# Two-layer transformer kernel, experts' pass: the down product ahead of the turn back, expert numbers read two at a time, the first batch's mix on VectorE, ten table entries moved to the heads

## What is computed

```
x = x + L0_attn(layernorm(x))     # gated recurrence of 6 heads
x = x + L0_ffn(layernorm(x))      # 2 shared experts + 16 routed experts, each token to its top 2
x = x + L1_attn(layernorm(x))     # causal attention, 16 heads of 128
x = x + L1_ffn(layernorm(x))      # gate, up, down weights = table[index], a table of 16 entries
```

```
routed[token] = sum over its 2 experts e of w[token, e] * (silu(x @ wg[e]) * (x @ wu[e])) @ wd[e]
```

## Time and profile before

| | |
|---|---|
| median of 3 runs | 2143.7 us (2142.53 to 2146.38) |
| the profiled execution's own time | 2146.1 us |
| span of the profiled execution | 2144.4 us, granted TensorE clock 0.993 |
| PE busy | 2080.2 us, 97% of the span |
| PEld busy | 1809.7 us, 84% |
| DVE busy | 1641.0 us, 77% |
| ACT busy | 1239.4 us, 58% |
| POOL busy | 590.2 us, 28% |

### The profile page before, as it was taken

One profiled execution on the slowest core, in us unless ns is written; L12 is line 12 of the kernel. 1 busy time (PEld: TensorE's weight loads), 2 busy tenths in 40 slices (PEclk: granted clock), 3 DMA queues, 4 the chain that ended last, 5 costly groups with the idle time before them and its releaser, 6 DMA issues. The chain is left out here.

```text
span 2144.4 us, 36740 instructions
## 1 busy us (share of the span) xinstructions
PE 2080.2 (97%) x12620; PEld 1809.7 (84%) x12620; DVE 1641.0 (77%) x4333; ACT 1239.4 (58%) x3432; POOL 590.2 (28%) x624
## 2 busy tenths in 40 slices
PE   6899999899999999999999999999999999999998
PEld 5777677577788999899899989988998999899887
DVE  6788787888878878768876777787687778767775
ACT  5443432236667666656665666666566666656662
POOL 3314354223133232223123311322231232112210
PEclk9999999999999999999999999999999999999999
DMA  6603021366422121113112211311221122111100
GB/s 193 205 1 104 33 77 48 150 191 199 144 74 60 45 75 55 40 43 97 40 41 71 68 40 40 91 43 44 66 70 40 40 79 60 40 50 45 41 20 20
DMA packets 92840, 154.56 MB, mean 72 GB/s; under 512 B 8688, under 2 KB 56560, under 8 KB 92656
## 3 DMA queue, kind: packets, MB, share of 16 engines
q1 hardware_dynamic: 72192, 121.53, 19.1%
q0 software_dynamic: 6144, 16.79, 2.4%
q10 hardware_dynamic: 14320, 13.90, 1.9%
HBM read 112.85 MB, written 39.32 MB: 71 GB/s over the span
## 5 line engine op out<-in xcount | busy, mean ns | idle before, releaser
L713 POOL TENSOR_TENSOR wo_low<-wraw_o,wo_high 128x256 fp32r<-128x256 f32 x128 | 95.1, 743 | 1141.2 <-ACT wo_high L777 1141.2
L1083 ACT ACTIVATE pr<-bank,negmax 128x128 f32<-128x128 f32 (+3 forms) x512 | 263.1, 527 | 195.4 <-DVE negmax L1645 195.4
L1203 DVE TENSOR_TENSOR p_low<-bank,p_high 128x512 fp32r<-128x512 f32 (+2 forms) x384 | 190.2, 551 | 101.5 <-ACT p_high L777 100.7
L777 ACT ACTIVATE p_high<-bank 128x512 fp32r<-128x512 f32 (+2 forms) x384 | 177.8, 497 | 149.6 <-PE bank L2208 149.6
L1645 DVE CUSTOM_DVE_ANT_0 bank<-bank,causal 128x128 f32<-128x128 f32 (+3 forms) x512 | 234.6, 520 | 1.1 <-PE bank L1832 1.1
L1672 DVE SCALAR_TENSOR_TENSOR xs<-bank,rinv,xs 128x256 f32<-128x256 f32 x512 | 211.7, 474 | 1.2 <-PE bank L1832 1.2
L1830 PE MATMUL bank<-h_high,wqk_high 128*128 128x512 f32 x512 | 202.6, 396 | 0.2 <-DVE h_low L1203 0.2
L1832 PE MATMUL bank<-h_high,wqk_low 128*128 128x512 f32 x512 | 202.5, 396 | 0.0
L1831 PE MATMUL bank<-h_low,wqk_high 128*128 128x512 f32 x512 | 202.4, 395 | 0.0
L1203 DVE TENSOR_TENSOR z_low<-bank,z_high 128x512 fp32r<-128x512 f32 x128 | 88.4, 691 | 130.8 <-ACT z_high L777 130.3
L703 POOL TENSOR_TENSOR wqk_low<-wraw,wqk_high 128x512 fp32r<-128x512 f32 x128 | 165.8, 1295 | 0.1
(11 more groups left out here) (349 smaller groups left out, 6185.8 us busy)
## 6 DMA issues: line engine op xcount, KB each, us to landing
wraw<-in_wpair SPq DMA_DIRECT2D x64, 512.0 KB, 4.0
wraw<-in_wpair SPq DMA_DIRECT2D x64, 256.0 KB, 4.3
wraw_o<-in_wpair SPq DMA_DIRECT2D x64, 256.0 KB, 2.9
tokens_by_expert<-xm SPq DMA_DIRECT2D x10, 1024.0 KB, 10.9
xt<-tokens_by_expert SPq DMA_DIRECT2D x40, 256.0 KB, 3.2
expert_results<-ey ACTq DMA_DIRECT2D x40, 256.0 KB, 3.7
wres<-in_wexp SPq DMA_DIRECT2D x1, 6144.0 KB, 19.7
xs<-x_between_stages SPq DMA_DIRECT2D x8, 512.0 KB, 4.9
```

Source lines behind the costliest of these rows:

```text
L713: pool.tensor_tensor(wo2[e][1][:], wraw_o[r][:, e, :], wo2[e][0][:].bitcast(F32), ALU.subtract).then_inc(s_wo, 1)
L777: sc.activation(dst, src, ACT.Copy, scale=scale).then_inc(done, 1)
L1083: ins = sc.activation(pr[:, i, 0:(i + 1) * P], score(i), ACT.Exp, scale=-1.0, bias=negmax[:, i:i + 1], accum_out=rsum[:, i:i + 1])
L1203: v.tensor_tensor(at(parts[1]), src, high_, ALU.subtract).then_inc(done, 1)
```

## The change

Six edits belong together:

- **PE's order.** In iteration t `tile_down(t-3)` now comes right behind `tile_gate_up(t-1)` (and behind the first batch's turn at t = 80), then the read of the expert numbers, then `tile_turn_back(t-2)`.
- **ACT's order.** `tile_result(t-3)` comes ahead of `tile_turned(t-2)`.
- **NVALUES** is 2 and not 4: 40 reads of two numbers in place of 20 reads of four.
- **The first batch's mix** moves from POOL to DVE, as 8 `scalar_tensor_tensor` at tiles 46 to 53. POOL's low parts of the first heads' weights now wait for the products `eh` of 52, 57, 62, 67 and 72 tiles (`s_ea`).
- **Table entries.** The pass goes up to entry 102 (`PASS_ENTRIES`) and not 112. Heads 0 to 9 now do two entries each, one ahead of `low_probs` and one behind `low_v`; heads 10 to 15 do one, as before. The seventh chunk's converted indices and compares get room in `fsg` and `ft` (bf16), since their old tiles are overlaid in the heads.
- **ACT's wait** in `high_ffn_weights`: for six chunks at n = 0, for seven at n = 6, for eight at n = 7.

```diff
-NVALUES = 4
+NVALUES = 2
+FIRST_MIX = 46
+FIRST_STATS = FIRST_MIX + 2 * NT + 2
+LOW_WEIGHTS = 52
+HEAD_ENTRIES = 10
+PASS_ENTRIES = LATE_CHUNK * LUTN - HEAD_ENTRIES
...
@@ pool
-            pool.wait_ge(s_x1[0], 16)
-            for c in range(2):
-                for i in range(NT):
-                    if c == 0:
-                        pool.wait_ge(s_yg[i], 32)
-                    linked(pool.tensor_scalar(yg[:, i, c, :], yg[:, i, c, :], wts[:, i, c:c + 1], None, ALU.mult))
-                for i in range(NT - 1):
-                    linked(pool.tensor_tensor(xs[0][:, i, :], xs[0][:, i, :], yg[:, i, c, :], ALU.add))
-                pool.tensor_tensor(xs[0][:, NT - 1, :], xs[0][:, NT - 1, :], yg[:, NT - 1, c, :], ALU.add
-                                   ).then_inc(s_mix, 1)
-                pool.wait_ge(s_mix, c + 1)
+            pool.wait_ge(s_ea, LOW_WEIGHTS)
             low_qk_weights(0, 0, 0)
+            pool.wait_ge(s_ea, LOW_WEIGHTS + 5)
             low_qk_weights(1, 1, 0)
+            pool.wait_ge(s_ea, LOW_WEIGHTS + 10)
             low_v_weights(0, 0)
+            pool.wait_ge(s_ea, LOW_WEIGHTS + 15)
             low_v_weights(1, 1)
+            pool.wait_ge(s_ea, LOW_WEIGHTS + 20)
             low_out_weights(0, 0, 0)
@@ scalar
-                if n in (0, LATE_CHUNK):
-                    sc.wait_ge(s_lut, (LATE_CHUNK + n // LATE_CHUNK) * LUTN)
+                if n in (0, LATE_CHUNK - 1, LATE_CHUNK):
+                    sc.wait_ge(s_lut, max(n + 1, LATE_CHUNK - 1) * LUTN)
...
+                if 0 <= t - 3 < NTILE:
+                    tile_result(t - 3)
                 if 0 <= t - 2 < NTILE:
                     tile_turned(t - 2)
-                if 0 <= t - 3 < NTILE:
-                    tile_result(t - 3)
@@ vector
             def equal_of(n):
-                return equal_late if n >= LATE_CHUNK * LUTN else equal[n % 2][:]
+                if n >= LATE_CHUNK * LUTN:
+                    return equal_late
+                return equal_bf_late if n >= PASS_ENTRIES else equal[n % 2][:]
...
                 if g < LUTN:
-                    unpack_to(LATE_CHUNK * LUTN + g + 1)
+                    unpack_to(PASS_ENTRIES + g + 1 + min(g, HEAD_ENTRIES))
                 low_probs(g)
...
                     low_v(g + 2, bank[5][:])
+                if g < HEAD_ENTRIES:
+                    unpack_to(PASS_ENTRIES + 2 * g + 2)
...
             def first_batch(t):
+                c, i = divmod(t - FIRST_MIX, NT)
+                if 0 <= c < 2:
+                    if c == 0:
+                        if i == 0:
+                            v.wait_ge(s_x1[0], 16)
+                        v.wait_ge(s_yg[i], 32)
+                    elif i == 0:
+                        v.wait_ge(s_mix, 1)
+                    ins = v.scalar_tensor_tensor(xs[0][:, i, :], yg[:, i, c, :], wts[:, i, c:c + 1], xs[0][:, i, :],
+                                                 ALU.mult, ALU.add)
+                    if i == NT - 1:
+                        ins.then_inc(s_mix, 1)
...
@@ tensor
+                if 0 <= t - 3 < NTILE:
+                    tile_down(t - 3, experts[t - 3])
                 if t < NTILE and t % NVALUES == 0:
                     experts += nc.values_load_multi_w_load_instructions(
                         expert_row[0:1, t:t + NVALUES], engines=(mybir.EngineType.PE,), min_val=0, max_val=NEXP - 1,
                         bass_reorder=False)[1]
                 if 0 <= t - 2 < NTILE:
                     tile_turn_back(t - 2)
-                if 0 <= t - 3 < NTILE:
-                    tile_down(t - 3, experts[t - 3])
```

More of the change, by code:

```diff
@@ L82 @@
 FIRST_TILES = 32
-FIRST_STATS = 56
+FIRST_MIX = 46
+FIRST_STATS = FIRST_MIX + 2 * NT + 2
+LOW_WEIGHTS = 52
 FIRST_CHAIN = FIRST_STATS + 4
@@ L245, in two_layer_program @@
         equal_late = fts[:, 0:LC]
+        fidx_bf_late = fsgs[:, LC:LC + LC // 2].bitcast(BF16)
+        equal_bf_late = fts[:, LC:LC + LC // 2].bitcast(BF16)
         wraw = [sb(f"wraw{i}", [P, 6 * D]) for i in range(2)]
@@ L1435, in unpack_index @@
                     v.wait_ge(s_leq, LUTN * (c - 1))
-                v.tensor_copy(fidx_bf[c % 2][:], fidxs[:, c, :]).then_inc(s_lidx, 1)
+                v.tensor_copy(index_of(c), fidxs[:, c, :]).then_inc(s_lidx, 1)
             def index_of(c):
-                return fidx_late if c == LATE_CHUNK else fidx_bf[c % 2][:]
+                return {LATE_CHUNK: fidx_late, LATE_CHUNK - 1: fidx_bf_late}.get(c, fidx_bf[c % 2][:])
             def equal_of(n):
-                return equal_late if n >= LATE_CHUNK * LUTN else equal[n % 2][:]
+                if n >= LATE_CHUNK * LUTN:
+                    return equal_late
+                return equal_bf_late if n >= PASS_ENTRIES else equal[n % 2][:]
             def unpack_equal(c, e):
@@ L1449, in unpack_equal @@
                     v.wait_ge(s_fidx[c % 2], 16 * (c // 2 + 1))
-                if c == LATE_CHUNK:
+                if n >= PASS_ENTRIES:
                     v.wait_ge(s_lut, n)
@@ L1780, in entries_until @@
             def entries_until(t):
-                busy = min(max(t + 1 - FIRST_STATS, 0), FIRST_APPLY + NT - FIRST_STATS)
+                busy = min(max(t + 1 - FIRST_MIX, 0), FIRST_APPLY + NT - FIRST_MIX)
                 weight = 2 * (t + 1) - busy
-                return (LATE_CHUNK * LUTN - early) * weight // (2 * NTILE - FIRST_APPLY - NT + FIRST_STATS)
+                return (PASS_ENTRIES - early) * weight // (2 * NTILE - FIRST_APPLY - NT + FIRST_MIX)
             def tile_product(t):
```

## The result

The changed kernel takes **2161.1 us** (median of 5 executions, 2160.0 to 2161.9), the kernel before 2143.7 (5 executions): a ratio of 1.008, 95% interval 1.0065 to 1.0095. It is slower, as forecast, but by 17.4 us where 5.5 were forecast, and lies above the range.

What follows compares the result with a forecast made beforehand. PE was taken as the bound, busy 2080.2 of 2144.4 us. Pass +4.9, its end +0.3 and heads +0.3 sum to 5.5 us: profiled 2151.6, less 2.4 for the median, 2149 us; overall range 2135 to 2153.

Steps and rivals of the forecast that it cites:

- The mechanism of the pass: PE's sequencer waits in order, so the last semaphore ahead of a read sets its lead; 0.34 us stall per read.
- a TENSOR_LOAD of two, I take 0.33, the row itself: Read in the pass: two numbers load as long as four, 0.33 us; 38 reads then cost 12.9 us.
- the shrinking read: Rival: a TENSOR_LOAD of two takes 0.165 us, pass 136.1, kernel 2141.6 us, no change; chance 0.25.
- the hidden read: Rival: reads in the pass are hidden, only slowed ones show; pass 129.4, kernel 2134.9 us; chance 0.20.
- Reads beside POOL: In the pass, four reads beside POOL's work cost 0.65 us more each: +2.6 us, bounds 0 to 4.6.
- the 0.6 taken off for the first read: In the pass, the first read, ahead of a filled pipeline, gets 0.6 us shorter.
- Both the 7.3 and the 2.7 us go: PE's standstill in the pass goes: 7.3 us between turns 39 and 54, 2.7 us at the reads.
- The end of the pass: Last tiles hang on successive ACT copies, one extra hand-over: +0.3 us, bounds 0 and 0.7.
- Ten entries in the heads: Heads 0 to 9 get one more entry each, mostly in DVE's idle time: +0.3 us; without cover 11 us.
- so seven or eight are hidden whole: Of ten entries in the heads, seven or eight fit DVE's idle time before `z_low`; short gaps lose 0.1 to 0.2.
- the heads pay: Rival: `z_low` comes late in all ten heads, up to 11 us, about 2159 us; chance 0.06.
- the pass at +4.9: The pass, turns of tiles 0 to 79, was to take 143.7 us against 138.8, +4.9.

Runs made afterwards that it cites:

- e16: The changed kernel with reads of one number and no second table entry in the heads: 2134.2 us, ratio 0.9952.
- e5: The kernel before with only the first batch's mix on DVE and POOL's later waits: 2146.7 us, ratio 1.0003.
- e2: The changed kernel with no second entries in the heads (112 in the pass): 2153.2 us, ratio 1.0046.
- e8: The kernel before with a read of four numbers at every second tile: 2174.2 us, one execution.
- e9: The kernel before with reads of eight numbers: 2168.9 us, ratio 1.011.
- e4: The kernel before with PE's and ACT's new order alone, reads of four, mix on POOL: 2153.8 us, ratio 1.0046.
- e1: The changed kernel with PE's and ACT's old order in the pass: 2159.9 us, ratio 1.0076.
- e17: The kernel before (old order) with the mix on DVE and reads of one number: 2140.0 us, ratio 0.9978.

## Why the prediction was wrong

**The mechanism of the pass was right, its size was not.** The new order makes the lead that hides a read depend on `ehT`; I laid its end at 0.65 behind the turn, it is 0.64, and the new place covers 0.65 us of a read where I had worked out 0.93 - 0.34 = 0.59. The term that failed is "a TENSOR_LOAD of two, I take 0.33, the row itself", with half of it as the other bound. It takes 0.54, above both ends: I had bounded it by a row of four as if fewer numbers could not take longer. The stall is 0.51 to 0.53 instead of 0.34, 38 reads cost 20 us and not 12.9. The rival of the shrinking read is refuted by the same row, and so is the hidden read. (The figure per register that the shrinking read takes from the Trainium skill, Runtime: NRT & Kernel Launch, Instruction fetch mechanics, is one for loads from HBM; `expert_row` lies in SBUF.)

The Trainium skill, DMA: Bandwidth & Descriptors, Latency and other measured facts, has a floor of about 600 ns, paid less often by unrolling by four. The traces do not bear out the floor: undisturbed loads take 0.30, 0.33 and 0.54 us. They agree that four at once is cheaper by the number, and an estimate with the page's 0.6 would have put the stall at 0.61, closer than mine. But unrolling is no rule in itself here: e16 shows one number in 0.30 us, hidden whole.

**"Reads beside POOL", +2.6: nothing.** The 39 loads of the changed kernel are all between 532 and 567 ns. The slow ones of the earlier trace rows start 0.81 to 1.10 us behind ACT's issue of a store, the other reads of before 0.53 to 0.57 behind it, and e5 has slow ones with POOL idle. So of the 4.7 us that the pass is longer than worked out (148.4 for 143.7), the stalls are +7.1 (20.0 for 12.9), the slow reads -2.6, and the rest is small: the 0.6 taken off for the first read does not show, and the floor is 0.4 lower (1.625 a step and not 1.63).

**"Both the 7.3 and the 2.7 us go": right.** In the changed kernel no step without a read is longer than 1.63 us, tiles 46 to 60 included, and in e16, where reads hide nothing, the one late product from tile 4 on is that of tile 64's step.

**The end of the pass, +0.3: nothing** (e2: 25.7 as before).

**Ten entries in the heads, +0.3: they cost 9.4.** This is the largest miss, and the step is "so seven or eight are hidden whole". I compared an entry's 1.1 us with a mean idle time of 1.24 us. But in that very idle time POOL subtracts, and the earlier trace rows had shown a DVE add at 1.67 beside POOL's subtractions; I used it for the mix and not here. There the entry takes up to 3.1 us. The rival "the heads pay" (up to 11 us, chance 0.06) had the place and nearly the price, but not the reason: the entry starts right behind `low_v`, as planned, and is itself longer, and heads 1, 3 and 9 hide it. That its 2159 lies near the measured 2161.1 is in part luck, since it holds the pass at +4.9 where 9.6 were measured (and by its own terms it is 2160). The Trainium skill, GPSIMD Engine Reference, Specifications, says that GpSimd's SBUF interfaces are shared with VectorE and contend with VectorE's instructions that have two SBUF inputs or run in its two-port mode; the add has two, and the runs agree: 0.78 alone, 1.75 beside POOL, while `z_low`, which reads one input from a bank, stays at 0.69.

Together: +9.6 in the pass (forecast 4.9) and +9.4 behind it (0.6) are 19.0 us between equal stage ones; the medians show 17.4.

**What stays open.** A TENSOR_LOAD in flight about a microsecond behind the issue of a store takes 0.2 to 0.9 us more. What it and the transfer share, no run here shows, and so it is not shown either that the store is the cause and not something that goes with it. Distance, count and POOL alone do not decide it (e8, e9, e5); the registers of gate and up are neither shown nor refuted.

## What to carry over

A sequencer's read of values costs its engine only what exceeds the lead at its place: work out the lead from the last wait ahead of it, measure the read at that very count, start and place, and make it short enough (one number at a time, 0.64 us, is free here behind a lead of 0.65). Idle time of DVE is worth its length only where POOL is idle too, so take an instruction's price from a row with the same neighbour. When lengths alternate, look at addresses and at what the other queues issue just before, ahead of any theory about the engine itself. Judge the parts of a change together with the sizes that go with them: in the pass, the new order lost 8.4 us with reads of four (e4), 2.5 with reads of two (the changed kernel against e1), and gained 5.3 with reads of one (e16 against e17).

## What was not expected of the hardware

- TENSOR_LOAD from SBUF on PE's sequencer: 0.30 us for one number, 0.54 for two, 0.33 for four that start at a multiple of four and 1.00 for four that start two behind one.
- A load of one, or of four from a multiple of four, that starts 0.66 to 1.41 us behind ACT's issue of a store takes 0.52 to 1.09 us (35 of 35); outside that it takes 0.30 to 0.36, with one exception in 280.
- After a read's standstill of 1.8 to 1.9 us the granted clock fell to 1.2 GHz for 3.4 us in four places of e9's pass.
- A DVE compare of 128 x 544 in bf16 goes from 0.29 to 1.32 us beside POOL's tensor operations, and the add from 0.78 to 1.75; an entry of 1.1 us becomes 3.1 in heads 0 and 6.
- Tile 0's turn, behind an unchanged stage one, starts anywhere from 444.4 to 452.9 us.
